# A macaron block on one core: the second feed-forward takes its rows from fixed regions per expert, in three routed groups

## The chip, the core and the metric

The kernel runs on one core of one Trainium2 chip. The metric is the device time of one execution in microseconds (us). TensorE (PE in the profile) multiplies matrices and transposes, VectorE (DVE), ScalarE (ACT) and GpSimd (POOL) do the elementwise work, SyncE (SP) issues plain DMAs, and GpSimd also issues the indirect DMAs, which scatter or gather rows of DRAM by a list of indices in SBUF.

## What is computed

x is [4, 1024, 128]: 4096 tokens of 128 features. Three steps follow each other, each on a layer norm of x:

```
x = x + 0.5 * ffn(layernorm(x))
x = x + attention(layernorm(x))      # cosformer, 16 heads of 64
x = x + 0.5 * ffn(layernorm(x))

def ffn(x):                          # x is already the layer norm
    weights = softmax(x @ gate_w.T + expert_bias)          # 8 experts
    top_w, top_i = top_k(weights, 2)
    top_w = top_w / (sum(top_w) + 1e-6)
    out = sum over the two chosen experts e of top_w[e] * (gelu(x @ w_up[e].T) @ w_down[e].T)   # 512 wide
    return layernorm(out) + x
```

## The kernel before

**Tokens.** There are 32 tiles of 128 tokens; four tiles are a block (512 tokens), eight blocks are the input. Precision is kept by splitting each fp32 operand into a high and a low fp16 part, so that one product is three matrix multiplications.

**A feed-forward.** It is done in two halves of 16 tiles. For each half VectorE works out the softmax and the two choices (`gating`, lines 489 to 548, ten pieces j) and from them the slot of each token's row (`route`, lines 566 to 606). Slots of an expert are padded to a multiple of 256 within the half. GpSimd scatters each tile's rows twice, once for each choice, into the DRAM tensor `xs` (`scatter`, line 636: 32 indirect DMAs a half). SyncE then loads 256 rows at a time, a pair, and each half has 23 pairs (NPAIR), whose experts PE reads from `tile_e`. A pair goes through transposes on PE (line 735), a copy on VectorE (838), 12 `up` products on PE (750 to 752), gelu and the high part on ACT (817 and 822), the low part on VectorE (842), 24 `down` products on PE (765 to 767), and a copy out on VectorE (849), after which SyncE stores the pair to `ys` (952). After a half's last pair has been stored, GpSimd gathers the two result rows of each token (line 665, eight indirect DMAs a block). VectorE weighs and adds them, normalises (`combine`, lines 674 to 698, with a power of -0.5 on GpSimd, line 672) and adds the result to x (`finish_apply`, lines 700 to 710). Before that, GpSimd has added the layer norm itself to x in pieces of 16 tiles (`add_input`, line 643).

**Attention.** Each of the 8 blocks n takes 8 steps hp, two heads in each, 64 steps in all. A step runs round PE, VectorE, ACT and GpSimd; on GpSimd it is the low part of q (line 1394), the low part of the running state in two instructions (1397, 1398), and the next step's q times the trigonometric rows in two instructions (1376). On VectorE the line 1292 (low part of the scores) opens the part of a step in which `beside` places other work: the layer norm of block n-1, which belongs to the second feed-forward, and in the first five blocks the rest of the first feed-forward. Line 1368 adds the attention of block n-1 to x in step hp 0, and GpSimd adds the output bias (line 1382) right behind. The gating of the second feed-forward's first half is spread over block 5, its `route` stands in block 6, step 0, and its 32 scatters follow on GpSimd from block 6, step 1, four in the first of these steps and two in each of the other 14. The gating and route of the last half wait for block 7, and so stand in the second feed-forward itself, behind pairs 3 to 6 of its first half.

**Order.** Each engine takes its instructions in the order in which they are written, with waits on semaphores between engines. PE's programs are `ffn_pe`, `attention_pe`, `ffn_pe`, and the other engines' likewise.

## Time and profile before

| | us |
|---|---|
| median of 3 runs | 1244.48 (1243.95 to 1246.01) |
| the profiled execution | 1245.46 |
| its span, first to last instruction | 1243.6 |
| first gelu of the second feed-forward | 1006.66 |
| last gelu of the second feed-forward | 1175.81 |

A profile shows one execution. Times are us from the start of the span unless marked ns. A busy share is an average over stages that have different limits, so each stage has to be read by itself. In the timeline a row has the start, the duration, the engine, the line, the operation, what it writes and reads, how many were merged, and in brackets how long the engine was idle before it and what ended that.

### The profile page before, as it was taken

How to read it: one execution, taken by the hardware profiler on the slowest of the kernel's cores; microseconds unless marked ns; L12 is line 12 of the kernel's file. 1: busy time of each engine (PE TensorE's matmuls, PEld its weight loads, DVE VectorE, ACT ScalarE, POOL GpSimd, SP SyncE). 2: the span in 40 equal slices, each digit the busy share in tenths (PEclk: the TensorE clock that was granted, in tenths of full speed). 3: DMA queues.
4: the chain of work that ended last, by engine and by line, in shares of the span. 5: the costliest groups of instructions: out<-in, count | busy, mean ns of one | idle time of the engine just before them, and what ended most of it. 6: DMA issues, size and time to landing. Idle time of an engine off the chain costs nothing.

```text
span 1243.6 us, 32918 instructions
## 1 busy us (share of the span) xinstructions
PE 926.5 (74%) x12872; PEld 753.5 (61%) x12872; DVE 1007.5 (81%) x2109; ACT 708.2 (57%) x1014; POOL 765.4 (62%) x635
## 2 busy tenths in 40 slices
PE   3302989778988878878879888977978877969800
PEld 2302988665766756656657666755756656958700
DVE  7887787897889899899899898898898857648933
ACT  2111767647766666666666775755757646746600
POOL 2187735816876766757756565547887822768264
PEclk9999999999999998999999999988999978989955
DMA  9322424320000000000000000000000012334231
GB/s 336 132 110 74 140 79 110 99 58 6 8 9 8 8 6 8 8 7 8 8 6 2 2 2 2 2 1 15 15 14 15 16 47 67 118 101 125 73 92 51
DMA packets 69508, 61.77 MB, mean 50 GB/s; under 512 B 8304, under 2 KB 60016, under 8 KB 69104
## 3 DMA queue, kind: packets, MB, share of 16 engines
q1 hardware_dynamic: 60448, 42.64, 11.2%
q0 software_dynamic: 8192, 16.79, 4.3%
q8 instruction: 109, 1.79, 0.6%
q14 instruction: 39, 0.32, 0.1%
q10 hardware_dynamic: 720, 0.23, 0.1%
HBM read 30.80 MB, written 28.84 MB: 48 GB/s over the span
## 4 chain that ended last, share of the span: by engine, by line
DVE 28%; POOL 27%; PE 20%; issue 16%; ACT 6%; DMA 2%; DVEq 0%; POOLq 0%; SPq 0%; ACTq 0%
POOL xs L636 8%; POOL arena_a L1394 5%; POOL arena_b L665 5%; DVE arena_b L1292 4%; POOL arena_a L1376 4%; DVE arena_a L1250 3%; ACT arena_c L1170 3%; PE bank L1060 3%; DVE arena_c L1288 2%; DVE arena_c L842 2%; POOL arena_c L1398 2%; DVE xn_new L426 2%; PE bank L984 2%; DVE arena_b L1275 2%; PE bank L750 2%
## 5 line engine op out<-in xcount | busy, mean ns | idle before, releaser
L636 POOL DMA_INDIRECT xs<-xhl,slot_idx x128 | 155.9, 1218 | 89.1 <-issue 56.9
L817 ACT ACTIVATE arena_c<-bank,s_pre 128x1024 f32<-128x1024 f32 x92 | 102.4, 1113 | 156.4 <-PE bank L752 151.1
L1394 POOL TENSOR_TENSOR arena_a<-arena_a 128x1024 f16<-128x1024 f32 x64 | 139.4, 2178 | 52.3 <-ACT arena_a L1170 51.7
L1376 POOL TENSOR_TENSOR arena_a<-arena_b,trig_rows 128x512 f32<-128x512 f32 x128 | 160.1, 1272 | 6.8 <-issue 6.8
L1170 ACT ACTIVATE arena_c<-arena_a 128x1024 f16<-128x1024 f32 x64 | 67.6, 1057 | 156.7 <-DVE arena_a L1250 156.7
L665 POOL DMA_INDIRECT arena_b<-ys,slot_idx x96 | 106.0, 1104 | 71.5 <-DMA ys<-arena_b 43.9
L765 PE MATMUL bank<-wdn_hi,arena_c 128*128 x736 | 132.2, 223 | 19.6 <-DVE arena_c L842 19.6
L842 DVE SCALAR_TENSOR_TENSOR arena_c<-arena_c,s_h 128x1024 f16<-128x1024 f32 x92 | 125.0, 1359 | 21.0 <-ACT arena_c L822 20.8
L766 PE MATMUL bank<-wdn_hi,arena_c 128*128 x736 | 132.1, 223 | 0.0
L767 PE MATMUL bank<-wdn_lo,arena_c 128*128 x736 | 131.9, 223 | 0.0
L1275 DVE TENSOR_TENSOR arena_b<-bank,decay 128x512 f32<-128x512 f32 x128 | 82.4, 686 | 40.8 <-PE bank L1060 40.2
L1170 ACT ACTIVATE arena_b<-arena_b 128x512 f16<-128x512 f32 x128 | 77.9, 630 | 64.3 <-DVE arena_b L1275 64.3
L822 ACT ACTIVATE arena_c<-arena_c,s_h 128x1024 f16<-128x1024 f32 x92 | 105.6, 1148 | 3.0
L750 PE MATMUL bank<-arena_b,wup_hi 128*128 128x256 f16 x368 | 104.4, 284 | 1.8 <-DVE arena_b L838 1.1
L751 PE MATMUL bank<-arena_b,wup_hi 128*128 128x256 f16 x368 | 104.3, 283 | 0.0
L752 PE MATMUL bank<-arena_b,wup_lo 128*128 128x256 f16 x368 | 104.2, 283 | 0.0
L1397 POOL TENSOR_TENSOR arena_c<-arena_c 128x130 f16<-128x130 f32 x64 | 34.4, 537 | 107.8 <-ACT arena_c L1220 107.5
L1292 DVE TENSOR_TENSOR arena_b<-arena_b 128x1024 f16<-128x1024 f32 x64 | 98.3, 1536 | 0.1
L1250 DVE SCALAR_TENSOR_TENSOR arena_a<-bank,trig_cols 128x512 f32<-128x512 f32 x128 | 82.2, 683 | 18.1 <-PE bank L986 17.1
L984 PE MATMUL bank<-wo_hi,arena_c 128*128 128x128 f16 x256 | 49.7, 229 | 60.8 <-DVE arena_c L1259 60.7
L765 PEld LDWEIGHTS bank<-wdn_hi,arena_c 128*128 128x128 f16 x736 | 73.7, 100 | 22.2 <-issue 21.1
L1288 DVE SCALAR_TENSOR_TENSOR arena_c<-bank,arena_c 128x130 f32<-128x130 f32 x256 | 74.5, 291 | 11.9
(227 smaller groups left out, 3721.8 us busy)
## 6 DMA issues: line engine op xcount, KB each, us to landing
arena_b<-xs SPq DMA_DIRECT2D x92, 128.0 KB
ys<-arena_b SPq DMA_DIRECT2D x92, 128.0 KB
xs<-arena_c SPq DMA_DIRECT2D x2, 3072.0 KB, 18.3
arena_a<-in_w_up SPq DMA_DIRECT2D x1, 2048.0 KB, 12.9
arena_b<-in_w_down SPq DMA_DIRECT2D x1, 2048.0 KB, 13.8
xs<-xhl,slot_idx POOLq DMA_INDIRECT x128, 2.3
out_x<-x_tok SPq DMA_DIRECT2D x8, 256.0 KB, 2.8
arena_b<-ys,slot_idx POOLq DMA_INDIRECT x96
```

The costliest lines, as they stand in the source:

```text
L636: nc.gpsimd.indirect_dma_start(d["xs"][half], bass.IndirectOffsetOnAxis(slot_idx[:, half, choice, t:t + 1], axis=0), xhl[:, half, t, :], N ...
L665: nc.gpsimd.indirect_dma_start(rows_of(q)[:, t, choice, :], None, d["ys"][half], bass.IndirectOffsetOnAxis(slot_idx[:, half, choice, at:at ...
L750: nc.tensor.matmul(dst, w_hi, x_hi, start=True, stop=False)
L765: nc.tensor.matmul(dst, hi, w_hi, start=(c + s == 0), stop=False, skip_group_check=True)
L766: nc.tensor.matmul(dst, lo, w_hi, start=False, stop=False, skip_group_check=True)
L767: i = nc.tensor.matmul(dst, hi, w_lo, start=False, stop=(c + s == CH), skip_group_check=True)
L842: nc.vector.scalar_tensor_tensor(h_lo[G % 4], h32[G % 2], s_h[:, 0:1], h_hi[G % 4], ALU.mult, ALU.subtract).then_inc(f["lo_done"], 1)
L1170: nc.scalar.activation(dst, src, ACT.Copy, scale=scale).then_inc(done, 1)
L1250: i = nc.vector.scalar_tensor_tensor(to[:, :, g, :], keys, 0.0, trig, ALU.max, ALU.mult)
L1292: nc.vector.tensor_tensor(probs_lo, probs, probs_hi, ALU.subtract).then_inc(a["probs_lo_done"], 1)
L1376: i = nc.gpsimd.tensor_tensor(q_trig[h], q_relu[h], trig_rows[:, bass.ds(u * BLK, BLK)], ALU.mult)
L1394: nc.gpsimd.tensor_tensor(q_lo, arena_a[:, 0:2 * BLK], q_hi, ALU.subtract).then_inc(a["q_lo_done"], 1)
```

## The change

The second feed-forward gets functions of its own (`second_pe`, `second_act`, `second_dve`, `second_pool`, `second_sync`); the first keeps the old ones.

- A DRAM tensor `xs2` has a region of 4096 rows for each expert. A row is 520 bytes: 256 fp16 values, the row's place in the result, and its weight. SyncE fills it with blank rows (34816 rows in 8 DMAs) at the start of attention.
- Tokens are routed in three groups, of 16, 8 and 8 tiles. For each, `route_next` continues the slots of each expert where the group before ended. After the second group it lists the full pairs; after the third the rest. There are 39 pairs (SECOND), of which the first 17 (FULL) need only the first two groups.
- The first group is gated in block 5, steps 0 to 3, and routed in step 4, and scattered from block 5, step 5 on: two scatters in each of three steps, four in each of block 6's steps 0 to 4, two in steps 5 to 7. The second is gated from block 6, step 6, to block 7, step 1, routed in block 7, step 2, and scattered in steps 3 to 7: two, two, four, four, four. The third is gated and routed in the second feed-forward at pairs 2 to 5, and its 16 scatters stand on GpSimd behind the results of pairs 0 to 3.
- ACT no longer copies the layer norm; it writes a twin of each row instead (`twin`). GpSimd adds the layer norm to x block by block (`add_input`, step hp 3 of the next block), straight from VectorE's buffer, and the next layer norm waits for that.
- VectorE scales a pair's results by their weight, and GpSimd scatters them to `ys2`, two indirect DMAs a pair, from a ring of 7 buffers. After all have landed, SyncE loads the two contributions of each block with plain DMAs (16 of 256 KB), VectorE adds them and takes the statistics, GpSimd takes the power and a product, ACT applies both, and GpSimd adds the result to x.

```diff
+CAP, ROW, NROWS = NTOK, 2 * D + 4, E * NTOK + 2048
+GROUPS = ((0, 16, 0), (16, 8, 16), (24, 8, 0))
+FULL = -(-(2 * P * 24 - E * (2 * P - 1)) // (2 * P))
+SECOND = NTOK * TOPK // (2 * P) + E - 1
+NXS, NYS, NIX = 6, 7, 12
...
+            if turn(r, n) and LN_ORDER[turn(r, n) - 1][0]:
+                v.wait_ge(f["x_sum"], 2 + LN_ORDER[turn(r, n) - 1][1] + 1)
...
-                nc.scalar.activation(xnh[:, n * TPB:(n + 1) * TPB, :], xn_new[:], ACT.Copy).then_inc(ln_hi, 1)
...
+        def twin(act, n):
+            act.wait_ge(xhl_lo, 2 + n + 1)
+            rows = source(source_of(n), TPB)
+            nc.scalar.activation(rows[:, :, 1, 0:2 * D], rows[:, :, 0, 0:2 * D], ACT.Copy).then_inc(twin_done, 1)
...
+        def add_input(g, n):
+            g.wait_ge(ln_norm, turn(1, n) + 1)
+            x = x_tok[:, n * TPB:(n + 1) * TPB, :]
+            nc.gpsimd.tensor_tensor(x, x, xn_new[:], ALU.add).then_inc(f["x_sum"], 1)
...
-                    for j in ((0,), (), (1, 2), (3, 4), (5, 6), (7,), (8,), (9,))[hp]:
+                if n == 5 and hp < 4:
+                    for j in ((0,), (1, 2, 3), (4, 5, 6), (7, 8, 9))[hp]:
                         gating(v, 2, j)
-                if n == 6 and hp == 0:
-                    route(v, 2)
+                if n == 5 and hp == 4:
+                    route_next(v, 0)
+                at = NHP * (n - 6) + hp - 6
+                if 0 <= at < 4:
+                    for j in ((0,), (1, 2, 3), (4, 5, 6), (7, 8, 9))[at]:
+                        gating(v, 3, j)
+                if n == 7 and hp == 2:
+                    route_next(v, 1)
...
-                            scatter(g, 2, (at + 1,) if at else (0, 1))
+                        at = NHP * (n - 5) + hp - 5
+                        if 0 <= at < 11:
+                            scatter_next(g, 0, ((0,), (1,), (2,), (3, 4), (5, 6), (7, 8), (9, 10), (11, 12), (13,), (14,),
+                                                (15,))[at])
+                        if n == 7 and hp > 2:
+                            scatter_next(g, 1, ((0,), (1,), (2, 3), (4, 5), (6, 7))[hp - 3])
...
+        def second_dve(v):
...
+            def take_y(p):
+                v.wait_ge(f["down_done"], G + 1)
+                if p >= NYS:
+                    v.wait_ge(out_y2[p % NYS], 32 * (p // NYS))
+                for s in range(2):
+                    i = nc.vector.tensor_scalar(y_sb2[p % NYS][:, s, :], ps_y[G % 2][:, s * D:(s + 1) * D],
+                                                meta[:, s, D + 1:D + 2], None, ALU.mult)
...
+                if p == 4:
+                    for j in range(1, GATE_PIECES):
+                        gating(v, 4, j)
+                if p == 5:
+                    route_next(v, 2)
...
+        def second_pool(g):
...
+            for p in range(BEFORE_LAST):
+                scatter_y(p)
+            scatter_next(g, 2, range(GROUPS[2][1]))
+            for p in range(BEFORE_LAST, SECOND):
+                scatter_y(p)
+            for b in range(NBLK):
+                power(b)
+                if b:
+                    add(b - 1)
+            add(NBLK - 1)
...
+        BEFORE_LAST = 4
+
+        def second_sync(sp):
...
+            for slot in range(NYS):
+                sp.wait_ge(out_y2[slot], 32 * len([p for p in range(SECOND) if p % NYS == slot]))
+            for b in range(NBLK):
+                for choice in range(2):
+                    rows = d["ys2"][choice * NTOK + b * BLK:choice * NTOK + (b + 1) * BLK, :]
+                    sp.dma_start(yl[b][:, choice, :, :], rows.rearrange("(t p) f -> p t f", p=P)).then_inc(in_yl[b], 16)
```

## Rows read from the trace of the kernel before

**Rows 1.** The page: the span; VectorE's line 842: xcount, busy us, mean ns, idle before

```profile
span 1243.6 us, 32918 instructions
L842 DVE SCALAR_TENSOR_TENSOR arena_c<-arena_c,s_h 128x1024 f16<-128x1024 f32 x92 | 125.0, 1359 | 21.0 <-ACT arena_c L822 20.8
```

**Rows 2.** Busy time by stretch, steady pairs: stretch, length, PE, PEld, DVE, ACT, POOL

```profile
1052.00:1087.00 35.00, 35.00 (x493) 33.36 (x490) 24.62 (x37) 27.63 (x26) 27.68 (x25) 1.00 0.41 125
```

**Rows 3.** Timeline, ACT: gelu of pairs 0, 9, 22, 23 and 45

```profile
1006.66 1.11 ACT L817 ACTIVATE arena_c<-bank,s_pre 128x1024 f32<-128x1024 f32 x1 [6.06 <-PE bank L752]
...
1051.26 1.11 ACT L817 ACTIVATE arena_c<-bank,s_pre 128x1024 f32<-128x1024 f32 x1 [0.58 <-PE bank L752]
...
1088.39 1.11 ACT L817 ACTIVATE arena_c<-bank,s_pre 128x1024 f32<-128x1024 f32 x1 [0.36 <-PE bank L752]
...
1107.24 1.12 ACT L817 ACTIVATE arena_c<-bank,s_pre 128x1024 f32<-128x1024 f32 x1 [16.56 <-PE bank L752]
...
1175.81 1.12 ACT L817 ACTIVATE arena_c<-bank,s_pre 128x1024 f32<-128x1024 f32 x1 [0.35 <-PE bank L752]
```

**Rows 4.** Timeline, GpSimd: the bias of block 5, 6 and 7

```profile
833.86 1.27 POOL L1382 TENSOR_TENSOR x_tok<-x_tok,bo_row 128x512 f32<-128x512 f32 x1 [8.96 <-DVE x_tok L1368]
...
921.28 1.28 POOL L1382 TENSOR_TENSOR x_tok<-x_tok,bo_row 128x512 f32<-128x512 f32 x1 [1.93 <-DVE x_tok L1368]
...
1001.90 1.26 POOL L1382 TENSOR_TENSOR x_tok<-x_tok,bo_row 128x512 f32<-128x512 f32 x1 [6.38 <-DVE x_tok L1368]
```

**Rows 5.** Timeline, GpSimd in attention: four scatters, and a step with two

```profile
843.06 1.08 POOL L636 DMA_INDIRECT xs<-xhl,slot_idx  x1 [0.20 <-issue]
...
847.11 0.96 POOL L636 DMA_INDIRECT xs<-xhl,slot_idx  x1 [0.30 <-issue]
...
872.24 2.15 POOL L1394 TENSOR_TENSOR arena_a<-arena_a 128x1024 f16<-128x1024 f32 x1
...
882.31 2.14 POOL L1394 TENSOR_TENSOR arena_a<-arena_a 128x1024 f16<-128x1024 f32 x1
```

**Rows 6.** Timeline, VectorE in attention, beside the four scatters

```profile
847.50 7.43 DVE L1292 TENSOR_TENSOR arena_b<-arena_b 128x1024 f16<-128x1024 f32 x1
```

**Rows 7.** Timeline, VectorE: gating pieces 1 to 9, then route

```profile
1034.95 0.28 DVE L516 TENSOR_REDUCE gcol<-gw 128x16 f32<-128x128 f32 x1
...
1040.48 0.69 DVE L546 TENSOR_TENSOR rt_mask<-gsel,gt 128x128 bf16<-128x128 f32 x1
...
1042.86 0.28 DVE L581 COPY rt_tot<-bank 128x128 f32<-128x128 f32 x1
...
1048.26 0.17 DVE L605 CAST tile_e<-rt_pack 128x3 int32<-128x3 f32 x1
```

**Rows 8.** Timeline, GpSimd in the second feed-forward: an addition, first and last of 32 scatters

```profile
1012.78 4.77 POOL L643 TENSOR_TENSOR x_tok<-x_tok,xnh 128x2048 f32<-128x2048 f32 x1
...
1049.20 2.00 POOL L636 DMA_INDIRECT xs<-xhl,slot_idx  x1 [31.64 <-DVE tile_e L605]
...
1094.28 0.96 POOL L636 DMA_INDIRECT xs<-xhl,slot_idx  x1 [0.30 <-issue]
```

**Rows 9.** DMA issues: what, count, KB each, median us to landing

```profile
xs<-xhl,slot_idx POOLq DMA_INDIRECT x128, 2.3
```

**Rows 10.** Timeline, all engines, the end of the span

```profile
1203.97 0.94 POOL L665 DMA_INDIRECT arena_b<-ys,slot_idx  x1 [0.30 <-issue]
...
1232.91 0.87 DVE L691 BATCH_NORM_STATS2 fst<-zt 128x6 f32<-128x128 f32 x4
1233.82 0.38 DVE L695 BATCH_NORM_AGGREGATE fmv<-fst 128x2 f32<-128x6 f32 x4
...
1234.48 1.01 POOL L672 TENSOR_TENSOR frstdh<-fvar,minus_half 128x4 f32<-128x4 f32 x1 [5.63 <-DVE fvar L698]
...
1236.67 0.69 DVE L710 TENSOR_TENSOR x_tok<-x_tok,zt 128x512 f32<-128x512 f32 x1
```

**Rows 11.** Groups by line and form, ACT: xcount, busy us, mean ns, idle before

```profile
L1219 ACT ACTIVATE arena_c<-arena_c 128x130 f16<-128x130 f32 x64 | 19.8, 309 | 0.6 <-DVE arena_c L1288 0.6
```

More of the change, by code:

```diff
@@ L550, in gating_exp @@
         def gating_exp(act, i):
-            tiles = slice((i % 2) * HALF, (i % 2 + 1) * HALF)
+            tiles = gate_tiles(i)[0]
             act.wait_ge(gate_in, i + 1)
@@ L975, in last_step, with clear_next @@
+        def clear_next(sp):
+            sp.wait_ge(blank_step, 2)
+            rows = d["xs2"].rearrange("(n t p) f -> n p t f", n=8, p=P)
+            for n in range(8):
+                sp.dma_start(rows[n], blank[:].unsqueeze(1).to_broadcast([P, NROWS // (8 * P), ROW // 2])).then_inc(blank_in, 16)
         def last_step(n):
@@ L1233, in attention_act @@
                                 gating_exp(act, 2)
+                        if n == 6 and hp == 6:
+                            gating_exp(act, 3)
+                        if hp == 6:
+                            if n > 0:
+                                twin(act, n - 1)
                         if hp == 7:
```

402 lines of the change are left out of this document (362 added, 40 removed).

## The prediction

> **What bounds the kernel now.** I read the page first, then the timeline stage by stage. The page gives the span, 1243.6 us [rows 1], and no engine that is busy through all of it, so the limit has to be found by stage. The profiled run took 1245.46, so 1.9 lie outside its span, and it is 1.0 above the median of the runs, 1244.48. My sum is made against the profiled run and lowered by 1.0 at the end.
>
> The second feed-forward, from its first gelu at 1006.66 to the end, lasts 236.9. While pairs follow each other undisturbed, PE is busy 35.00 of 35.00 us and the others are not [rows 2]; 13 pairs from gelu 9 to gelu 22 take 37.1, so a pair costs 2.86 and PE sets it [rows 3]. The rest is waiting. Gelu 0 to 9 takes 44.6 in place of 25.7. Between the halves, gelu 22 to 23, stand 18.85 (the scatters of the last half have to land). The second half's 22 steps take 68.6 in place of 62.9, since the finish of the first half's blocks lies between them. From the last gelu to the end it is 67.8: store, 32 gathers on GpSimd for the last four blocks, the finish, the output.
>
> In attention the work goes round the engines step by step. With two scatters a step, GpSimd runs without a gap and a step takes 10.07 from one low part of q to the next [rows 5]. From bias to bias, block 6 takes 87.4 and block 7 takes 80.6, both with 16 or 18 scatters [rows 4]; so two scatters a step can hide. But behind the four scatters GpSimd worked on without a gap and held VectorE's line 1292 for 7.43 [rows 6]. On this stage the change loads more work.
>
> **The change, part by part.**
>
> *Second feed-forward: pairs.* 39 pairs in place of 46 take off 7 x 2.86 = 20.0. The wait between the halves goes: 18.85 - 2.86 = 16.0. The finishes among the pairs go: 5.6.
>
> *Its start.* VectorE's gating pieces 1 to 9 ran from 1034.95 to 1041.17 and route from 1042.86 to 1048.43, 6.2 and 5.6 [rows 7]. With 8 tiles in place of 16 I estimate 5.2 for gating and 6.8 for the longer `route_next` (52 - 31 = 21 chained steps), so together as much as before. What goes is the addition of 16 tiles on GpSimd, 4.77 [rows 8], beside which VectorE's layer norm was stretched. Following the queues pair by pair, I get gelu 9 at 39 after gelu 0 in place of 44.6: 5.6 less. The first loads wait for the scatters of block 7's last step, four in place of two: 1.6 more, counted under attention.
>
> *The result ring.* This is the new wait. GpSimd starts the third group's 16 scatters about 28.5 after gelu 0, when their slots are known. The 32 scatters of before took (1094.28 - 1049.20) / 31 = 1.454 each beside running pairs [rows 8]; without VectorE's interference a gather costs 0.94 + 0.30 = 1.24 [rows 10], and I take that for the lower end. So 16 take 23.3, to 51.8; only then come the results of pair 4. VectorE wants buffer 11 % 7 = 4 again at about 52, and gets it when pair 4 has been written and has landed: 51.8 + 2.9 + 2.3 [rows 9] = 57. It waits some 4.5, and PE, whose down products need the emptied bank, and SyncE's loads, which wait for y_used, stand behind it. From there two scatters a pair cost 2 x 1.454 = 2.91, about PE's 2.86, so GpSimd hardly catches up and stays 7 pairs behind. Gelu 38 is at 39 + 29 x 2.86 + 4.5 = 126.4. GpSimd ends at 51.8 + 28 x 2.91 + 7 x 2 x 1.24 = 150.6, and the last row lands at 152.9.
>
> The Trainium skill (GPSIMD Engine Reference, section 8, Key points) says that GpSimd shares SBUF interfaces with VectorE and contends with VectorE instructions that have two SBUF inputs. `low` (line 842) is such an instruction; 1.454 against 1.24 agrees in direction. If each `low` held the scatters for its whole length, a pair would cost more, which is the fourth rival.
>
> *The end.* Now all eight blocks come after the last scatter. Per block: aggregate 0.38 [rows 10], two small VectorE instructions 0.35, power 1.01 [rows 10], a product on 4 columns about 0.3 (an estimate below the power), ACT four times 0.31 [rows 11], the steps between engines about 0.4: 3.7 in a loop, since the next aggregate waits for ACT. The sum (0.69), the statistics (0.87) of the next block [rows 10] and the last addition (1.27 on GpSimd, as the bias of the same size [rows 4]) lie beside it. First loads about 3.4 (over 2.3 for 64 KB, these are 512 KB [rows 9]); the other 3.5 MB stream behind, since 125 GB/s used 0.41 of the DMA engines [rows 2] and 512 KB a block in 3.7 is 142 GB/s. In all 3.4 + 0.69 + 0.87 + 8 x 3.7 + 1.27 = 35.8, and the way from the last addition to the end is 1243.6 - 1237.4 = 6.2 [rows 1, 10]: 42.0. So 152.9 + 42.0 = 194.9 against 236.9: **42.0 less** (39 saved on the pairs and waits, 5.6 - 4.5 at start and ring, and an end 68.5 long in place of 67.8; rounding takes the rest).
>
> *Attention.* Block 5 to 6: gating and routing as before, route shorter by 1.9, the first six scatters hidden: nothing. Block 6 to 7: five steps now have four scatters. Two more cost 2.5 to 3.2 in a GpSimd step that already had no gap (four took 5.0, with the first at 843.06 and the last to 848.07 [rows 5]): 14. Part of the second group's gating on VectorE, 4.4, and the block addition, 1.3. From a bare 80.6 that is 100.3, against 87.4: 12.9. Block 7 to the end: the rest of that gating 2.2, `route_next` with the full-pair list 6.8, two four-scatter steps 5.7, the addition 1.0, the late first load 1.6: 17.3. All VectorE work counts fully, because it stands in `beside`, ahead of the products of the step. In blocks 1 to 5, the addition of one block on GpSimd (1.27 each) and the twin on ACT (longer than the copy that it replaces) have idle time to lie in; I bound them by 0 and 8 and take 4. The wait of the layer norm for that addition costs nothing: three steps lie between; if GpSimd fell that far behind, VectorE and all its queue would stand. The 18 MB of blank rows run on SyncE's queue from the start of attention, ahead of nothing until the first pair; they can delay the gathers of the first feed-forward's late blocks: 0 to 5, taken as 1. Sum: **35 more**.
>
> 1245.5 - 42.0 + 35 = 1238.5, less 1.0: about 1238.
>
> **The rivals.**
> 1. *Attention hides it.* Block 7 of before took 80.6 with its 16 scatters, as little as a bare block. If four a step hide too, 15 to 20 of the 35 go: 1220. Against it: no gap is left in a step with two [rows 5].
> 2. *Slower: GpSimd's bursts hold VectorE.* The step behind the four scatters lost some 6 to the 7.43 stall [rows 6]. There are seven such steps now with work behind them, and half of them stalling so gives about 20 more: 1258. It decides once attention grows by over 42. For it: it happened in the only four-scatter step that there is. Against: when GpSimd is the bound anyway, the stall falls into time already counted.
> 3. *The ring doesn't bind.* If scatters cost 1.24 each, GpSimd catches up 0.38 a pair, and ends about 10 sooner: 1228.
> 4. *The ring binds harder.* With each `low` holding GpSimd for all of its 1.36 [rows 1], a pair costs 2 x 1.24 + 1.36 = 3.84: 28 x 0.93 = 26 more, 1264. The 1.454 speaks against it.
> 5. *It doesn't do what it says.* The third group lands too late for pair 17, and a wait like that between the halves (16) returns: 1254. Its scatters end at 51.8 by my sum and pair 17's load is due about then; six buffers of lead speak against it.
>
> **How the numbers follow.** Forecast 0.36, rivals in order 0.22, 0.24, 0.10, 0.06, 0.02. The likeliest gives 1238, by itself 1228 to 1247. The range takes in attention from 20 to 55 more and a second feed-forward of 32 to 52 less, not both ends at once: 1214 to 1262. A difference of 0.2% (2.5 us) is about what a measurement can tell from none. Faster is most of the forecast's own range with rivals 1 and 3: 0.58. Within 0.2% is a third of the forecast's upper side: 0.13. Slower is rivals 2, 4, 5 and the rest: 0.29.
>
> **What would show it.** Right: gelus of the second feed-forward 2.86 to 2.95 apart after the start, a wait of VectorE for DMA `ys2` near pair 11, scatters running some 17 beyond the last `low`, and a loop of about 3.7 a block at the end; the low parts of q 12.5 to 13.3 apart in the four-scatter steps, and blocks 6 and 7 near 100 long. Wrong: blocks 6 and 7 under 90 (rival 1) or over 110 with VectorE instructions of 5 us and more (rival 2), or scatters 1.9 apart (rival 4).

## The result: slower by 0.6%

The changed kernel takes 1253.55 us (median of 14 executions, 1246.99 to 1259.11) against 1245.49 for the kernel before, beside it on the same chips: a ratio of 1.0056, 95% interval 1.0036 to 1.0077. I had forecast 1238, faster. The profiled execution took 1255.69, 1.8 of it outside its span, and the numbers by stage below are from its trace. The page of after, its span, data rates (40 slices of 31.3 us), and the group of the result scatters:

```profile
span 1253.9 us, 32419 instructions
...
GB/s 337 131 109 73 141 84 118 92 76 185 196 188 9 8 9 8 6 9 8 6 8 2 2 2 2 1 15 22 23 15 2 6 17 49 62 80 96 78 165 59
...
L1321 POOL DMA_INDIRECT ys<-arena_b,row_at x78 | 84.8, 1087 | 36.3 <-issue 22.6
```

The 185, 196 and 188 GB/s in slices 10 to 12 are the blank rows. In before the same slices move 6, 8 and 9 GB/s.

**Attention** is read at GpSimd's bias, which stands right behind each block's addition. Blocks 4 to 7 in after:

```profile
749.31 1.27 POOL L1812 TENSOR_TENSOR x_tok<-x_tok,bo_row 128x512 f32<-128x512 f32 x1 [1.95 <-DVE x_tok L1798]
...
849.01 1.28 POOL L1812 TENSOR_TENSOR x_tok<-x_tok,bo_row 128x512 f32<-128x512 f32 x1 [1.92 <-DVE x_tok L1798]
...
952.27 1.27 POOL L1812 TENSOR_TENSOR x_tok<-x_tok,bo_row 128x512 f32<-128x512 f32 x1 [5.21 <-DVE x_tok L1798]
...
1048.39 1.26 POOL L1812 TENSOR_TENSOR x_tok<-x_tok,bo_row 128x512 f32<-128x512 f32 x1 [2.08 <-DVE x_tok L1798]
```

Before has its block 4 here, and blocks 5 to 7 in [rows 4]:

```profile
740.61 1.27 POOL L1382 TENSOR_TENSOR x_tok<-x_tok,bo_row 128x512 f32<-128x512 f32 x1 [1.92 <-DVE x_tok L1368]
```

So the last three blocks take 99.7, 103.3 and 96.1 in after, and 93.3, 87.4 and 80.6 in before.

**Second feed-forward**, ACT's gelus of pairs 0, 9, 14 to 18 and 38 in after, answering [rows 3]:

```profile
1055.34 1.11 ACT L1233 ACTIVATE arena_c<-bank,s_pre 128x1024 f32<-128x1024 f32 x1 [8.25 <-PE bank L1183]
...
1092.14 1.11 ACT L1233 ACTIVATE arena_c<-bank,s_pre 128x1024 f32<-128x1024 f32 x1 [0.58 <-PE bank L1183]
...
1106.51 1.11 ACT L1233 ACTIVATE arena_c<-bank,s_pre 128x1024 f32<-128x1024 f32 x1 [0.58 <-PE bank L1183]
1113.38 1.11 ACT L1233 ACTIVATE arena_c<-bank,s_pre 128x1024 f32<-128x1024 f32 x1 [4.58 <-PE bank L1183]
1116.25 1.11 ACT L1233 ACTIVATE arena_c<-bank,s_pre 128x1024 f32<-128x1024 f32 x1 [0.58 <-PE bank L1183]
1124.17 1.11 ACT L1233 ACTIVATE arena_c<-bank,s_pre 128x1024 f32<-128x1024 f32 x1 [5.62 <-PE bank L1183]
1128.33 1.11 ACT L1233 ACTIVATE arena_c<-bank,s_pre 128x1024 f32<-128x1024 f32 x1 [1.87 <-PE bank L1183]
...
1185.57 1.11 ACT L1233 ACTIVATE arena_c<-bank,s_pre 128x1024 f32<-128x1024 f32 x1 [0.35 <-PE bank L1183]
```

VectorE's waits from 1090 to 1140 (us in total, times, longest), the last of the 78 result scatters, the first sum of the end, and the last rows of the span:

```profile
DVE arena_b L1273 <- DMA ys<-arena_b,row_at: 9.2, 3, 6.0
```

```profile
1202.94 0.96 POOL L1321 DMA_INDIRECT ys<-arena_b,row_at  x1 [0.31 <-issue]
...
1208.92 0.69 DVE L1300 TENSOR_TENSOR arena_a<-arena_a 128x512 f32<-128x512 f32 x1 [17.41 <-DMA arena_a<-ys]
...
1235.35 0.38 DVE L1310 BATCH_NORM_AGGREGATE fmv<-fst 128x2 f32<-128x6 f32 x4 [2.03 <-ACT arena_c L1246]
...
1236.08 1.39 POOL L1327 TENSOR_TENSOR frstdh<-fvar,minus_half 128x4 f32<-128x4 f32 x1 [1.30 <-DVE fvar L1314]
...
1237.79 1.65 ACT L1246 ACTIVATE arena_c<-arena_c,shift,frstdh 128x128 f32<-128x128 f32 x4 [2.54 <-POOL shift L1329]
1239.53 0.38 DVE L1310 BATCH_NORM_AGGREGATE fmv<-fst 128x2 f32<-128x6 f32 x4 [2.03 <-ACT arena_c L1246]
...
1243.32 1.26 POOL L1334 TENSOR_TENSOR x_tok<-x_tok,arena_c 128x512 f32<-128x512 f32 x1 [0.55 <-ACT arena_c L1246]
```

Between the first gelus of the two traces lie 1055.3 - 1006.7 = 48.7 us, the growth of all that comes ahead; from the first gelu to the end it is 198.5 in place of 237.0, 38.4 less. Together 10.2, which is the difference of the spans. From block to block, before and after, with the prediction's figures:

| stage | before | after | difference | predicted |
|---|---|---|---|---|
| attention to block 4's addition (blocks 0 to 4) | 451.9 | 462.0 | +10.1 | +5 |
| block 5 | 93.2 | 99.7 | +6.5 | 0 |
| block 6 | 87.4 | 103.3 | +15.9 | +12.9 |
| block 7 and up to the first gelu | 86.3 | 104.0 | +17.7 | +17.3 |
| first gelu to the end | 237.0 | 198.5 | -38.4 | -42.0 |

(The attention itself began 1.4 earlier, at 286.3 in place of 287.7.)

### The profile page after: what moved, and what is told of

It is laid out like the page before. It is cut to its first block, busy times and chain, and to the rows that moved or that the text cites. A ratio compares the mean times of both kernels' runs of the same rounds, so it can differ in the third digit from the quotient of the medians.

```text
span 1253.9 us, 32419 instructions
## 1 busy us (share of the span) xinstructions
PE 917.1 (73%) x12594; PEld 745.9 (59%) x12594; DVE 985.5 (79%) x2130; ACT 711.1 (57%) x1033; POOL 790.1 (63%) x671
## 4 chain that ended last, share of the span: by engine, by line
DVE 26%; POOL 25%; PE 23%; issue 14%; ACT 7%; DMA 3%; DVEq 0%; POOLq 0%; SPq 0%; ACTq 0%
POOL arena_a L1824 5%; DVE arena_b L1716 5%; POOL xs L782 4%; POOL xs L814 3%; DVE arena_a L1674 3%; PE bank L1477 3%; POOL arena_a L1806 3%; ACT arena_c L1589 3%; DVE arena_c L1712 2%; POOL arena_b L843 2%; PE bank L1401 2%; POOL arena_c L1828 2%; DVE xn_new L477 2%; PE bank L1403 2%; PE bank L1402 2%
## 5 line engine op out<-in xcount | busy, mean ns | idle before, releaser
L1321 POOL DMA_INDIRECT ys<-arena_b,row_at x78 | 84.8, 1087 | 36.3 <-issue 22.6
L814 POOL DMA_INDIRECT xs<-xhl,slot_idx x64 | 78.5, 1227 | 40.4 <-issue 40.4
L995 ACT ACTIVATE arena_c<-bank,s_pre 128x1024 f32<-128x1024 f32 x46 | 51.2, 1113 | 92.2 <-PE bank L930 86.5
L1477 PE MATMUL bank<-arena_b 64*128 64x128 f32 x1024 | 85.9, 315 | 0.0
L1477 PEld LDWEIGHTS bank<-arena_b 64*128 64x128 f32 x1024 | 72.7, 215 | 15.7 <-issue 15.4
L1583 ACT ACTIVATE arena_b<-bank,bq_kept 128x512 f32<-128x512 f32 x128 | 80.7, 676 | 2.4 <-PE bank L1403 2.2
L1679 DVE TENSOR_TENSOR arena_c<-arena_a,arena_c 128x1024 f16<-128x1024 f32 x64 | 79.6, 1245 | 1.1 <-ACT arena_c L1589 1.1
L1401 PE MATMUL bank<-arena_c,arena_a 128*128 128x65 f16 x512 | 56.9, 198 | 26.7 <-POOL arena_c L1828 26.7
L1401 PEld LDWEIGHTS bank<-wo_hi,arena_c 128*128 128x128 f16 x256 | 27.5, 108 | 80.5 <-DVE arena_c L1683 69.4
L1020 DVE SCALAR_TENSOR_TENSOR arena_c<-arena_c,s_h 128x1024 f16<-128x1024 f32 x46 | 66.2, 1440 | 8.1 <-ACT arena_c L1000 8.1
L943 PE MATMUL bank<-wdn_hi,arena_c 128*128 x368 | 65.6, 222 | 7.7 <-DVE arena_c L1020 7.7
```

The source lines that it names most:

```text
L814: nc.gpsimd.indirect_dma_start(d["xs"][half], bass.IndirectOffsetOnAxis(slot_idx[:, half, choice, t:t + 1], axis=0), xhl[:, half, t, :], N ...
L1321: nc.gpsimd.indirect_dma_start(d["ys2"], bass.IndirectOffsetOnAxis(row_at[:, p % NIX, s:s + 1], axis=0), y_sb2[p % NYS][:, s, :], None).th ...
L1401: nc.tensor.matmul(dst, lhs[0], rhs[0], start=first, stop=False, skip_group_check=True)
L1477: i = nc.tensor.matmul(ps_so[:, h, cols], k_relu[rows, cols], q_relu[h][rows, cols], start=True, stop=True)
L1583: nc.scalar.activation(dst, ps_pj[(5 * hp + j) % 2], ACT.Relu, bias=bias, scale=FEATURE).then_inc(a["q_evac"], 1)
```

## The experiments

All are edits of the changed kernel, except one, which says so. Block windows are from addition to addition, as in the table; the first is counted from the first low part of q.

**Blank rows later.**

```
             sp.wait_ge(blank_step, 2)
+            sp.wait_ge(a["att_sum"], 5)
```

> The changed kernel, but SyncE writes the 18 MB of blank rows only after block 3's attention has been added to x, when the last gather of the first feed-forward has been used. Theory: those writes slow the gathers of blocks 0 and 1, and VectorE waits for them; then the way from the first low part of q to block 0's addition falls from 95.3 us to about 88.6 (as in the kernel before), the next block from 96.3 to 92.7, nothing else changes, and the time falls by about 10 to some 1243. Rival: the writes cost what they cost wherever they stand, by the traffic in SBUF and DRAM; then blocks 4 and 5 grow by 5 to 10 and the time stays.

Measured: 1248.47 us, ratio 1.0014 (0.9999 to 1.0029). Blocks 0 and 1 take 88.5 and 92.8, against 95.2 and 96.3 in after and 88.6 and 92.7 in before; the last three stay at 99.8, 103.4, 96.2. GpSimd's bias of block 1 is at 468.73 here and at 478.81 in after. In after VectorE waited for a gather of the first feed-forward, and in this run no such wait is listed (VectorE's waits, 286 to 480, after):

```profile
DVE zt L859 <- DMA xhl<-ys,slot_idx: 5.3, 1, 5.3
```

So the blank rows cost what blocks 0 and 1 gained. They are now written from 653.9 to 750.0, beside block 4, which takes 85.5 in place of 85.2, so there they cost next to nothing. In the trace of after the 10 us have two parts. One is the wait above. The other is an instruction of VectorE that ran for 6.21, where the same line took 1.22 in most steps. GpSimd's elementwise rows follow each other without a gap beside it, from 384.90 to 390.69:

```profile
385.57 6.21 DVE L1716 TENSOR_TENSOR arena_b<-arena_b 128x1024 f16<-128x1024 f32 x1
```

How much the blank rows cost varies. All nine traces with early blank rows have the wait, of 3.8 to 5.8; only three of them have an instruction held for over 6 in this stretch. The three traces with late ones have neither. Blocks 0 and 1 together took between 182.6 and 191.5 in the nine, and 180.1 to 182.3 in the three. The traced execution of after is the dearest of them; by the medians the price is some 5 us (0.42%), half of what the theory gave.

**No more than two scatters of the first group in a step.**

```
-    if 0 <= at < 11:
-        scatter_next(g, 0, ((0,), (1,), (2,), (3, 4), (5, 6), (7, 8), (9, 10), (11, 12), (13,), (14,), (15,))[at])
+    if 0 <= at < 14:
+        scatter_next(g, 0, ((0,), (1,), (2,), (3,), (4,), (5,), (6,), (7,), (8,), (9,), (10,), (11,),
+                            (12, 13), (14, 15))[at])
```

(Each entry is a tile, scattered twice; the last tiles fall into block 7.)

> The changed kernel, but the first group's scatters are spread over 14 steps (two in each of twelve, four in the last two) in place of 11 (four in each of five). Theory A, four scatters a step make GpSimd the bound: the way from block 5's addition to block 6's falls from 103.3 us by 8 to 12, block 7 grows by 3 at most, and the time falls by 5 to 9. Theory B, block 6's growth is VectorE's gating and its being held by GpSimd, whatever the number of scatters: within 3 us of the changed kernel.

Measured: 1251.14, ratio 1.0055 (1.0037 to 1.0073). Block 6 fell from 103.3 to 96.3, block 7 rose from 96.1 to 101.7; both together 198.0 in place of 199.4. The price went with the scatters to the next block. Neither theory holds as put: block 6 gained 7.0 where the first has 8 to 12, and block 7 lost 5.6 where it has 3 at most.

**No scatters in attention.**

```
-    if 0 <= at < 11:
+    if False:
...
-    if n == 7 and hp > 2:
+    if False:
```

(The waits for these scatters go with them, and the result rows are cleared once.)

> The changed kernel without the scatters of the first two groups (their rows stay blank, so the results of 24 tiles are missing), with their place in the result zeroed by one DMA in block 4. What is left of the growth of blocks 5 to 7 is then VectorE's gating and routing. Theory A, the 48 scatters are the price: the three stretches between additions fall from 99.7, 103.3 and 96.1 us to about 93, 88 and 88, some 30 together. Theory B, the gating and routing instructions on VectorE are held by GpSimd's ordinary work in attention: they fall to about 97, 92 and 93, some 17 together, and gating instructions of 0.2 us still take about 1 us.

Measured: 1222.68 in one execution. The biases of blocks 4 to 7:

```profile
744.38 1.27 POOL L1814 TENSOR_TENSOR x_tok<-x_tok,bo_row 128x512 f32<-128x512 f32 x1 [1.94 <-DVE x_tok L1800]
...
843.99 1.28 POOL L1814 TENSOR_TENSOR x_tok<-x_tok,bo_row 128x512 f32<-128x512 f32 x1 [1.92 <-DVE x_tok L1800]
...
927.76 1.27 POOL L1814 TENSOR_TENSOR x_tok<-x_tok,bo_row 128x512 f32<-128x512 f32 x1 [5.21 <-DVE x_tok L1800]
...
1011.39 1.26 POOL L1814 TENSOR_TENSOR x_tok<-x_tok,bo_row 128x512 f32<-128x512 f32 x1 [7.40 <-DVE x_tok L1800]
```

Block 5 takes 99.6 still, so its growth isn't the scatters'. Blocks 6 and 7 take 83.8 and 83.6: 32.0 less for 42 scatters, 0.76 each in the mean. The sum is near the 30 of theory A, but it lies in two blocks and not in three. Busy time over block 6, after and then this run (stretch, length, PE, PEld, DVE, ACT, POOL, granted clock, DMA share, GB/s):

```profile
849.00:952.00 103.00, 80.43 (x1121) 62.34 (x1119) 79.07 (x142) 59.60 (x100) 80.91 (x69) 0.89 0.06 18
```

```profile
844.00:928.00 84.00, 74.31 (x1153) 56.50 (x1150) 74.92 (x143) 58.91 (x100) 52.83 (x44) 1.00 0.01 2
```

GpSimd is busy 28 us longer, and about 8 more go in the 0.30 between its scatters, for 19 us of time, so part of it is hidden. What isn't comes in a few steps. PE's waits for GpSimd's low part of the running state, which stands on GpSimd's queue behind a step's scatters, over these two stretches (us in total, times, longest), after and then this run:

```profile
PE bank L1401 <- POOL arena_c L1828: 10.9, 7, 5.5
```

```profile
PE bank L1403 <- POOL arena_c L1830: 1.6, 8, 0.3
```

And VectorE's low part of the scores was held twice in after, in block 6 and in block 7, beside GpSimd's elementwise rows; without the scatters no instruction of VectorE in attention takes over 2.9:

```profile
867.70 7.03 DVE L1716 TENSOR_TENSOR arena_b<-arena_b 128x1024 f16<-128x1024 f32 x1
...
997.31 7.44 DVE L1716 TENSOR_TENSOR arena_b<-arena_b 128x1024 f16<-128x1024 f32 x1
```

TensorE's granted clock was 0.89 of the higher level in the mean of the stretch, in place of 1.00, where PE waited longer, and its products took 6 us more; how much of the 0.76 is that, these runs don't tell.

**The first group's gating and routing one block later**, without scatters as in the run above.

```
-    if n == 5 and hp < 4:
+    if n == 6 and hp < 4:
         for j in ((0,), (1, 2, 3), (4, 5, 6), (7, 8, 9))[hp]:
             gating(v, 2, j)
-    if n == 5 and hp == 4:
+    if n == 6 and hp == 4:
         route_next(v, 0)
```

(PE's `route_product` and ACT's exponential move with it.)

> The run without scatters in the attention (rows of the first two groups not carried over, that part of the output left out), and the first group's gating and routing moved from block 5 to the same steps of block 6. Without the move the three last block windows were 99.6, 83.8 and 83.6 us, where the kernel before has 93.2, 87.4 and 80.6. Theory (VectorE has no slack in block 5, where it also finishes the last block of the first feed-forward, and most of the 17 us of gating and routing lie on the path there; in blocks 6 and 7 it has slack, as block 7 took 14 us of gating and routing for 3 us more): block 5's window falls from 99.6 to 84 to 88, block 6's rises from 83.8 to 86 to 92, a gain of 4 to 11 us over both. Rival (VectorE has no slack in any of these blocks): block 6 rises by as much as block 5 falls, to 96 to 99, and nothing is gained.

Measured: 1213.43 in one execution, but not by this. The biases:

```profile
742.94 1.28 POOL L1813 TENSOR_TENSOR x_tok<-x_tok,bo_row 128x512 f32<-128x512 f32 x1 [1.92 <-DVE x_tok L1799]
...
822.19 1.27 POOL L1813 TENSOR_TENSOR x_tok<-x_tok,bo_row 128x512 f32<-128x512 f32 x1 [1.92 <-DVE x_tok L1799]
...
925.87 1.27 POOL L1813 TENSOR_TENSOR x_tok<-x_tok,bo_row 128x512 f32<-128x512 f32 x1 [5.21 <-DVE x_tok L1799]
...
1008.62 1.26 POOL L1813 TENSOR_TENSOR x_tok<-x_tok,bo_row 128x512 f32<-128x512 f32 x1 [6.75 <-DVE x_tok L1799]
```

Block 5 falls by 20.4 to 79.2, block 6 rises by 19.9 to 103.7. My theory that block 6 has slack falls; the rival holds. Packed as it is, this work lies on the path in full in either block: the 11.15 us of gating and 5.76 of routing (22 and 12 instructions of VectorE in after, their rows added up) cost about 20. The rest of the 1213.43 against 1222.68, 9 us, lies mostly in the second feed-forward, 198.9 from first gelu to end in place of 205.3. Its code is the same in both. The last scatter ends 149.2 behind the first gelu here and 155.7 in the run above, where ten of the result scatters came 2.0 to 2.3 behind the one before; in after it is 148.6. So that stretch came out long in the run above, and why stays open.

**The same work placed as the kernel before has it**, again without scatters.

```
-    if n == 5 and hp < 4:
-        for j in ((0,), (1, 2, 3), (4, 5, 6), (7, 8, 9))[hp]:
+    if n == 5:
+        for j in ((0,), (), (1, 2), (3, 4), (5, 6), (7,), (8,), (9,))[hp]:
             gating(v, 2, j)
-    if n == 5 and hp == 4:
+    if n == 6 and hp == 0:
         route_next(v, 0)
```

(PE's `route_product` goes to block 5, step 7.)

> The run without scatters in the attention (rows of the first two groups not carried over, that part of the output left out), with the first group's gating and routing placed as the kernel before has them: one or two pieces of gating in seven of block 5's steps, the routing in block 6, step 0, ahead of block 5's addition. Without the scatters and with the changed kernel's placement (up to three pieces a step in steps 0 to 3, routing in step 4) the windows of blocks 5 to 7 were 99.6, 83.8 and 83.6; before has 93.2 in block 5, with 17.6 us of gating and routing on VectorE against 16.9 in after, and a block without any took 79.2. Theory (one or two pieces fit in part into what VectorE has left over in a step, three don't; so the packing costs the 6.5): block 5's window falls to 92 to 94.5, block 6 and 7 stay within 1.5 of 83.8 and 83.6. Rival (the work itself grew more costly, by the rows' places and weights that gating now also writes and by the addition and the twin beside it): block 5 stays at 98 or above.

Measured: 1205.53 in one execution. The biases of blocks 4 and 5:

```profile
741.62 1.28 POOL L1816 TENSOR_TENSOR x_tok<-x_tok,bo_row 128x512 f32<-128x512 f32 x1 [1.93 <-DVE x_tok L1802]
...
832.66 1.28 POOL L1816 TENSOR_TENSOR x_tok<-x_tok,bo_row 128x512 f32<-128x512 f32 x1 [6.74 <-DVE x_tok L1802]
```

Block 5 takes 91.0 in place of 99.6; blocks 6 and 7 stay at 83.7 and 83.1. The theory holds, with 1 to 3.5 us more than it gave: about the same work (15.5 us of VectorE) costs 12 over the 79.2 when one or two pieces stand in a step, and 20 when three do. The routing moved together with the gating, and this run doesn't tell the two apart.

The runs without scatters also give a price for those of before. Before has 16 in block 6 and no gating there, and the block takes 87.4 [rows 4]; block 5 of the run above has neither, and takes 79.2. That is 8.2, or 0.51 each, and most of it lies in one step. VectorE's first product with the decay in a step, from step 1 to 3 in that block 5, and steps 2 and 3 of block 6 in before:

```profile
742.69 1.29 DVE L1700 TENSOR_TENSOR arena_b<-bank,decay 128x512 f32<-128x512 f32 x2
...
754.12 1.29 DVE L1700 TENSOR_TENSOR arena_b<-bank,decay 128x512 f32<-128x512 f32 x2 [0.34 <-PE bank L1479]
...
764.84 1.29 DVE L1700 TENSOR_TENSOR arena_b<-bank,decay 128x512 f32<-128x512 f32 x2 [0.34 <-PE bank L1479]
```

```profile
845.05 1.29 DVE L1275 TENSOR_TENSOR arena_b<-bank,decay 128x512 f32<-128x512 f32 x2 [0.34 <-PE bank L1060]
...
861.44 1.29 DVE L1275 TENSOR_TENSOR arena_b<-bank,decay 128x512 f32<-128x512 f32 x2 [1.27 <-PE bank L1060]
```

Step 2 takes 16.4 in place of 10.7: it is the step of the instruction held for 7.43 [rows 6]. The other seven steps cost 2.5 together, so two scatters a step are nearly hidden in this block, as I had read.

**The last addition on VectorE** (with nothing else changed; `add(b - 1)` moves from `second_pool` into `second_dve`'s loop).

> The changed kernel, but the last addition of each block, x plus result, is on VectorE in place of GpSimd. Theory: the program ends 9 us after GpSimd's last instruction, which is that addition; with the power's product as GpSimd's last instruction the end comes about 3 us earlier, though VectorE's part is not shorter, and the loop of 4.19 us a block keeps its length within 0.3. Rival: the output's store sets the end; then it gains 0.6 at most, the difference of 1.26 and 0.69 for the last addition.

Measured: 1252.35, ratio 1.0040 (1.0018 to 1.0063). From the last scatter to the end 47.4 in place of 50.0, near the 3 less that the theory gives; by the medians this run can't be told from after, since the intervals overlap. VectorE's last instruction ended at 1245.70, the span at 1252.6, 9.30 behind GpSimd's last instruction (1243.29): as in after, where GpSimd's last row ends at 1244.58 and the span at 1253.9, again 9.30. So I took GpSimd off the end altogether.

**GpSimd off the end.**

```
 # ScalarE, per block:
+    act.wait_ge(last_var, b + 1)
+    nc.scalar.activation(fvar4[:], fvar4[:], ACT.Sqrt).then_inc(last_pow, 1)
...
 # VectorE, per block, in place of GpSimd's power, product and addition:
+    v.wait_ge(last_pow, 2 * b + 1)
+    nc.vector.reciprocal(frstdh[:], fvar4[:]).then_inc(last_pow, 1)
+    v.wait_ge(last_pow, 2 * b + 2)
+    nc.vector.tensor_tensor(shift4[:], frstdh[:], neg_mean[:], ALU.mult).then_inc(last_line, 1)
+    if b:
+        add(b - 1)
...
```

> The changed kernel with GpSimd taken off the last normalization: the power becomes a square root on ScalarE and a reciprocal on VectorE, the shift's product and the last addition go to VectorE. GpSimd's last instruction is then its last scatter, some 50 us before the end. In after and in the run with only the last addition on VectorE the span ended 9.30 us after GpSimd's last instruction, and the output's last store had landed some 4 to 7 us before that end. Theory (the end waits for GpSimd's drain, 8 to 9 us after its last instruction): with the drain beside the loop, the span ends within 1 to 3 us of the last store's landing, and end minus last scatter falls from 49.9 to between 41 and 46 us. Rival (the tail belongs to the last store or to the program's end, whichever engine ran last): the end stays 6 to 9 us behind the last compute instruction or 4 us or more behind the store's landing, and end minus last scatter is at 47 to 50, as with the last addition on VectorE (47.4).

Measured: 1239.82, ratio 0.9947 (0.9925 to 0.9969), faster than both kernels. GpSimd's last row, two aggregates and the last addition; the span of this trace is 1233.4:

```profile
1195.52 0.96 POOL L1336 DMA_INDIRECT ys<-arena_b,row_at  x1 [0.30 <-issue]
...
1223.57 0.38 DVE L1316 BATCH_NORM_AGGREGATE fmv<-fst 128x2 f32<-128x6 f32 x4
...
1227.01 0.38 DVE L1316 BATCH_NORM_AGGREGATE fmv<-fst 128x2 f32<-128x6 f32 x4
...
1230.02 0.69 DVE L1281 TENSOR_TENSOR x_tok<-x_tok,arena_c 128x512 f32<-128x512 f32 x1 [1.11 <-ACT arena_c L1248]
```

The span ends 2.7 behind the last addition and 0.4 behind the landing of the last store (1233.0), which in after lies 7.0 ahead of the end (1246.9). It ends 37.0 behind the last scatter in place of 50.0. Of these 13, 6.6 are the end behind the last instruction (9.3 to 2.7), some 5.9 the loop (8 times 4.18 - 3.44), and 0.6 the addition (0.69 in place of 1.26). The theory holds, and the gain is larger than its 4 to 9, since the loop shrank too, which I hadn't counted.

**A longer ring.**

```
-NXS, NYS, NIX = 6, 7, 12
+NXS, NYS, NIX = 6, 12, 16
```

> The changed kernel with a ring of 12 buffers for the second feed-forward's results in place of 7 (and 16 sets of row numbers in place of 12); nothing else differs. After: VectorE waits for the ring in three places around pairs 15 to 18 (gaps of 6.9, 7.9 and 4.2 us between gelus where 2.87 is usual, 10.4 us more than without), last gelu 130.2 after the first, last scatter 148.6, so 18.4 us behind the last gelu. Theory (GpSimd's scatters set the end of the second feed-forward from the third group on, and the ring's wait is only where that shows): the gaps shrink and the last gelu comes 6 to 10 us earlier (120 to 124), but the last scatter stays at 147 to 149, and the time moves by less than 2 us. Rival (the ring's wait itself is what costs the 10.4 us, the scatters would keep up): the last scatter comes 8 to 10 us earlier too, at 139 to 141, and the time falls by 8 to 10 us.

Measured: 1252.49, ratio 1.0049 (1.0036 to 1.0062). VectorE no longer waits for the ring, and the last gelu comes 123.8 after the first in place of 130.2. The last scatter ends 150.9 after it (148.6 in after; 147 to 149 expected). The wait for the ring costs nothing: GpSimd's scatters set the end.

**No third group of scatters.** The call `scatter_next(g, 2, ...)` is left out of `second_pool`.

> The changed kernel without the 16 scatters of the third group (the last two blocks' rows are not carried over, so their part of the output is left out; the loads of the last pairs wait for the third group's slots in place of its scatters, and the result rows are cleared once so that what is loaded at the end is defined). Theory (GpSimd full, 16 x 1.24 to 1.45 = 20 to 23 us of its work taken away): no gap over 4 us between gelus, last gelu 119 to 122 after the first (130.2 in after), last scatter within 4 us of the last gelu plus one pair (123 to 127, where after has 148.6), so the second feed-forward is some 22 to 25 us shorter. Rival (the gaps come from the landing of the scatters and loads, not from GpSimd's own time): some of the gaps stay, and the last scatter comes under 12 us earlier.

Measured: 1238.67 in one execution. The waits for the ring are gone, the last gelu is at 121.1 as the theory says, and the last scatter ends at 131.9, 16.7 earlier; expected were 22 to 25. One gap of 4.2 between gelus stayed. GpSimd sets this stretch, but without the 16 scatters it stands idle where it waits for pair 4's result, so that not all of their time comes back.

**Late blank rows and GpSimd off the end together.** The two edits shown above.

> The changed kernel with two edits together: GpSimd taken off the last normalization (as in the run with the square root on ScalarE: 1239.8, its end 37.0 us behind the last scatter in place of 49.9) and the blank rows written after block 4's addition in place of the start of attention (that run: 1248.5 in place of 1253.6, blocks 0 and 1 back to 88.5 and 92.8). Theory (the two costs lie in different stages and add): 1253.6 - 13.7 - 5.1 = 1234.8, between 1232 and 1238, so 0.6 to 1.1% under the kernel before. Rival (the later blank rows now collide with the second group's scatters or with the first loads of the second feed-forward, and give back what they saved): 1238 to 1242, with blocks 5 to 7 or the start of the second feed-forward longer than 99, 103, 96 and 37 us.

Measured: 1235.87, ratio 0.9909 (0.9880 to 0.9938). They add, as the theory says.

**The spread gating in this version.** Late blank rows, GpSimd off the end, the gating and routing as before has them, and the first group's scatters from block 6, step 1, on:

```
-    at = NHP * (n - 5) + hp - 5
-    if 0 <= at < 11:
-        scatter_next(g, 0, ((0,), (1,), (2,), (3, 4), (5, 6), (7, 8), (9, 10), (11, 12), (13,), (14,), (15,))[at])
+    at = NHP * (n - 6) + hp - 1
+    if 0 <= at < 10:
+        scatter_next(g, 0, ((0,), (1,), (2, 3), (4, 5), (6, 7), (8, 9), (10, 11), (12, 13), (14,), (15,))[at])
```

> The version with late blank rows and GpSimd off the end (1235.9), and the first group's gating and routing placed as the kernel before has them, so that its scatters begin in block 6, step 1 (16 tiles over ten steps). In the run without scatters this placement took block 5 from 99.6 to 91.0. Six scatters of the first group, which block 5 hid, now fall into blocks 6 and 7, where 42 cost 0.76 each. Theory (both prices hold and add): block 5 at 91 to 93, blocks 6 and 7 together 4 to 5 longer than the 197.7 of that version, so 2 to 5 us less in all: 1231 to 1234. Rival (the scatters squeezed into fewer steps cost their full 1.26 each or delay the second group's, so that nothing is left of the gain): blocks 6 and 7 at 205 or more together, and 1235 to 1238.

Measured: 1227.02 (1223.53 to 1231.73), ratio 0.9847 (0.9820 to 0.9874): the best version found, 1.5% faster than the kernel before. Block 5 takes 92.2 in place of 99.2, blocks 6 and 7 together 197.7, as without the edit: the six scatters that now fall there cost nothing that shows, better than either theory. So 0.76 is a mean of steps that cost much and steps that cost nothing, and no price that can be carried to another placement. The medians differ by 8.9, of which block 5 explains 7.0.

**The kernel before, without GpSimd in its last two blocks' powers.**

```
-                finishing(q + 7, q + 6, None)
-                finish_power(g, q + 7)
+                finishing(q + 7, None, None)
...
 # ScalarE takes the root of fvar4 for q = 14 and 15, VectorE the reciprocal in finish_apply
```

> The kernel before, with only the powers of its last two finished blocks taken from GpSimd (a square root on ScalarE, a reciprocal on VectorE). GpSimd's last instruction is then the last gather, which ended at 1227.8 in the profiled run of before; its last power ended at 1235.49 and the span at 1243.65, 8.16 later, while VectorE's last addition ended at about 1237.4. Theory (the span waits for GpSimd's drain): the end goes to 2.5 to 3.5 us behind VectorE's last instruction, and the kernel gains 2.5 to 4.5 us (1241 to 1243), without any part of the change. Rival (the drain belongs to the new scatters to rows, or the 6 us behind the last addition to the store): no difference, 1245 to 1246.

Measured: 1239.15, ratio 0.9958 (0.9942 to 0.9974): 5.2 less, more than the 2.5 to 4.5 expected. The last gather and the last addition; the span of this trace is 1238.7:

```profile
1227.57 0.95 POOL L666 DMA_INDIRECT arena_b<-ys,slot_idx  x1 [0.30 <-issue]
...
1235.29 0.69 DVE L714 TENSOR_TENSOR x_tok<-x_tok,zt 128x512 f32<-128x512 f32 x1
```

Again 2.7 behind the last addition, where before had 6.2 [rows 1, 10]; that is 3.5, and from the first gelu to the last addition's end it is 2.6 less, by two powers without a hop to GpSimd and back. So the 8 to 9 us belong to GpSimd in either kernel, and not to the new scatters. With both kernels rid of them, the old one stands at 0.9958, and the changed one at 0.9947 as it is, at 0.9909 with its blank rows moved, and at 0.9847 with its gating spread too.

## Why the prediction was wrong

The sum was -42.0 + 35 = -7 and the traces gave -38.4 + 48.7 = +10.2. Of the 17.3 us between them 13.7 lie in attention and 3.6 in the second feed-forward. (The "39 saved on the pairs and waits" in the prediction is 41.6 by its own terms, 20.0 + 16.0 + 5.6; the 42.0 was worked out from the end and stands.)

**Block 5 (0 predicted, 6.5 measured): the packing was left out.** "Gating and routing as before ... nothing" took over the amount of work and not its place. The amount is the same: 9.88 of gating and 7.69 of routing on VectorE in before (that routing too stands ahead of block 5's addition), 11.15 and 5.76 in after. But before has one or two pieces of gating in a step, and the change has three. The run with the old placement took block 5 back to 91.0, and scatters have no part in it (99.7 with them, 99.6 without; that the first six hide was forecast). So the place costs 8.6, of which the shorter routing, forecast at 1.9, gives back 2.2 (91.0 against 93.2). That VectorE does part of one or two pieces while it waits for others, and can't with three, is inferred and not shown.

**Blank rows (1 predicted, 9 to 10 in this trace, 5 by the medians): a value that was too low.** I bounded them by 0 and 5 and took 1; the medians lie at the bound and this trace above it. The mechanism was in the text, that they can delay the gathers of the first feed-forward. What I didn't weigh is that they would fill the DMA engines at 185 to 196 GB/s for three slices, and that the block's finish on VectorE waits for a gather in this very stretch (5.3 here). What the trace has beyond that is the instruction held for 6.21. The addition and the twin in blocks 1 to 5, for which I took 4, cost nothing: with the blank rows out of the way, blocks 0 to 4 take 452.1 in place of 451.9.

**Blocks 6 and 7 (12.9 and 17.3 predicted, 15.9 and 17.7 measured): nearly the sum, and nearly its terms.** I set them against a "bare" 80.6 and put the added scatters at 19.7, VectorE's work at 13.4 and the two additions at 2.3. The blocks came near the 100 I gave, with the four-scatter steps 10.8 to 15.6 apart where I had 12.5 to 13.3. The 80.6 was not bare, since it held 16 scatters, but that moved the sum little. Without scatters, block 7 has the second group's gating and routing in steps 1 and 2. VectorE's first product with the decay in steps 1 and 3 there:

```profile
927.50 1.28 DVE L1701 TENSOR_TENSOR arena_b<-bank,decay 128x512 f32<-128x512 f32 x2
...
961.14 1.29 DVE L1701 TENSOR_TENSOR arena_b<-bank,decay 128x512 f32<-128x512 f32 x2 [0.34 <-PE bank L1479]
```

That is 33.6, against 22.1 in the block without either (742.69 to 764.84 above), so 11.5 are gating and routing. A bare block 7 would take 83.6 - 11.5 = 72.1, and before's 16 scatters cost 8.5 in it; with the 8.2 of block 6 that is some 17 for 32. The 42 of after cost 32. So some 15 of the growth of 31.4 from bias to bias are scatters, and some 16 are gating and routing: the 11.5, and in block 6 83.8 - 79.2 = 4.6. The addition of the layer norm on GpSimd, 2.27 in block 6 where I had 1.27, is in the 79.2 too and has no price of its own here. This split takes blocks of the changed kernel without scatters for before's; no run of before without scatters shows it by itself. On VectorE the second group's gating and routing take 11.55 + 8.03 us in after. My price for gating came from the second feed-forward, where it runs without GpSimd's elementwise work beside it. VectorE, one instruction with one input and one with two, first in block 6 of attention and then in the second feed-forward, both in after:

```profile
931.44 0.22 DVE L602 TENSOR_REDUCE gcol<-gw 128x8 f32<-128x64 f32 x1
931.69 0.94 DVE L604 TENSOR_TENSOR gt<-gw,gcol 128x64 f32<-128x64 f32 x1
...
1073.69 0.22 DVE L602 TENSOR_REDUCE gcol<-gw 128x8 f32<-128x64 f32 x1
1073.95 0.22 DVE L604 TENSOR_TENSOR gt<-gw,gcol 128x64 f32<-128x64 f32 x1
```

The one with two inputs takes four times as long in attention. The 22 instructions of gating took 11.55 us there and 4.99 in the second feed-forward, where I had estimated 5.2. The Trainium skill (GPSIMD Engine Reference, section 8, Key points) says that GpSimd contends with VectorE instructions in a two-port mode or with two SBUF inputs; the rows agree, and show the size.

**The ring (+4.5 predicted, 10.2 measured): right in place, and without effect.** The third group's scatters made room at 51.5 after the first gelu (51.8 predicted), and VectorE waited for `ys2` behind pair 11, for longer than I said: from gelu 9 to 38 it took 93.4, and 29 undisturbed steps of 2.87 are 83.2. But I took the end from GpSimd, 150.6, and it came at 148.6. The longer ring shows that VectorE's wait isn't on the path. The start was better than forecast (gelu 9 at 36.8, forecast 39), and so was the pace of scatters: 1.26 and 1.61 in turn, 2.87 a pair where I had 2.91.

**The end (44.3 behind the last scatter predicted, landing included; 50.0 measured): more than the miss of this stage.** The loop took 4.18 a block where I had 3.7: the power 1.39 beside VectorE's addition in place of 1.01, and the four ACT instructions 1.65 in place of 1.24, which was the price of another form on ACT [rows 11]. Eight of these are 3.8. And behind the last addition I put the 6.2 that before has there. That was a gap measured from VectorE's last instruction; it is ruled by GpSimd's, which ended 8.16 ahead of the span's end in before. With the last addition on GpSimd it became 9.3: 3.1 more. The first loads came sooner than I said: the first sum begins 5.0 behind the last scatter, where I had 5.7.

**The rivals.** The second, slower at 1258 by GpSimd's bursts, had its sign right and its condition, attention over 42 longer. That its 1258 is near the result is chance. Its mechanism occurs, but is not the growth: VectorE was held for 7.03 and 7.44 in two steps of blocks 6 and 7, and in before for 7.43 [rows 6] and 5.44 (at 925.9) in two. Nor does it need four scatters in a step: with two in each of block 6's steps VectorE was still held there, for 5.43 and 7.38, and the price only moved to the next block. The first, that attention hides it, falls with 103 and 96 for its blocks; the third with the scatters at 2.87 a pair; the fourth with the same number against 3.84. The fifth didn't occur: pair 17's load waited 4.5 for the third group, which is part of the 10.2 that cost nothing. The time, 1253.55, lies inside the range. The direction was wrong: faster stood at 0.58.

## What to carry to other kernels

Work moved to another step costs what that step has no room for, so price it by its place and not by its amount, from rows with the same engines at work beside it, and check that a stage taken as bare is bare. Look at which engine ends last, not only when: keep GpSimd out of the last 10 us of a kernel. Large transfers that nobody waits for belong in a stretch where nobody waits for a small one either.

## What the hardware showed unexpectedly

- The span ended 8.0 to 9.3 us behind GpSimd's last instruction in each of the runs where that was among the last, and 2.7 behind VectorE's last instruction in the four where GpSimd had ended 10 us or more before the end (10.2, 36.8, 36.8, 37.0). What GpSimd does in that time the profile doesn't show. It was 9.30 or 9.31 in five runs with 270 indirect DMAs, 8.64 in three with 222, 8.16 with 256, and 8.0 with 254.
- In the second group's gating, beside GpSimd's wide elementwise rows, eight of VectorE's instructions that take 0.22 us in the second feed-forward took 0.46 to 1.19; all have two SBUF inputs. Those with one input stayed at 0.20 to 0.22, and so did, at 0.23, two with two inputs beside GpSimd's power on 4 columns.
- An instruction of VectorE that takes 1.22 us took 6.21 to 7.44 in three steps of after (385.57, 867.70, 997.31), in which GpSimd's elementwise rows followed each other without a gap beside it.
- A scatter that GpSimd issues took 1.26 from one to the next alone, and 1.26 and 1.61 in turn beside VectorE's work on running pairs (after).
